# Causal mask, negation and row maximum of attention scores fused into one VectorE instruction per head and query tile, in place in PSUM

## What is computed

```python
scores = jnp.einsum('bqhd,bkhd->bhqk', qh, kh) / jnp.sqrt(jnp.float32(hd))
scores = jnp.where(causal[None, None, :, :], scores, -jnp.inf)
weights = jax.nn.softmax(scores, axis=-1)
out = jnp.einsum('bhqk,bkhd->bqhd', weights, vh).reshape(B, S, D)
```

## Time and profile before

| | us |
|---|---|
| median of 3 runs | 1448.44 |
| lowest and highest | 1437.71, 1454.72 |
| the profiled execution's own time | 1450.46 |
| its span in the trace | 1448.7 |
| TensorE matmuls busy | 1228.7 (85%) |
| TensorE weight loads busy | 1045.6 (72%) |
| VectorE busy | 904.6 (62%) |
| ScalarE busy | 557.8 (39%) |
| GpSimd busy | 626.0 (43%) |

### The profile page before, as it was taken

How to read it: one execution, slowest core, us unless ns; L and a number is a source line. 1 busy time by engine, 2 the same in 40 slices (tenths; PEclk the granted TensorE clock), 3 DMA queues, 4 the chain that set the end, 5 groups by cost and what they waited for, 6 DMA issues and landing times.

```text
span 1448.7 us, 33276 instructions
## 1 busy us (share of the span) xinstructions
PE 1228.7 (85%) x12722; PEld 1045.6 (72%) x12722; DVE 904.6 (62%) x2063; ACT 557.8 (39%) x959; POOL 626.0 (43%) x996
## 2 busy tenths in 40 slices
PE   1488999999999999999999997648997878979874
PEld 1366777777777777777777766548996768979874
DVE  2376767777877778688688685567874323434331
ACT  0124444443444443434434443234452334545431
POOL 3123333334544444444344443416326555645564
PEclk7799999999999999999999998769997889989987
DMA  3201112113223232232232212487666555857630
GB/s 113 83 19 49 47 38 72 48 51 111 89 83 102 82 101 84 82 110 81 82 104 79 86 63 76 157 301 249 234 239 175 178 178 178 269 196 260 207 127 26
DMA packets 84230, 177.73 MB, mean 123 GB/s; under 512 B 16370, under 2 KB 57594, under 8 KB 84070
## 3 DMA queue, kind: packets, MB, share of 16 engines
q1 hardware_dynamic: 70406, 146.73, 31.4%
q0 software_dynamic: 13664, 28.84, 5.6%
HBM read 128.96 MB, written 50.38 MB: 124 GB/s over the span
## 4 chain that ended last, share of the span: by engine, by line
PE 40%; DVE 20%; issue 14%; POOL 11%; ACT 6%; DMA 4%; SPq 3%; another core or an unknown queue 1%; POOLq 0%; DVEq 0%; ACTq 0%
PE h_ps L1615 9%; PE y_ps L1626 9%; DVE capped L974 4%; ACT PT L738 3%; PE round_banks L582 3%; POOL sorted_d L226 3%; DVE xn L990 3%; PE gen L502 3%; POOL PT L852 3%; DVE nm L978 2%; PE round_banks L555 2%; PE gen L544 2%; PE gen L511 2%; DVE nm L976 2%; POOL rstd L845 2%
## 5 line engine op out<-in xcount | busy, mean ns | idle before, releaser
L738 ACT ACTIVATE PT<-round_banks 128x1752 f32<-128x1752 f32 x96 | 156.6, 1632 | 174.8 <-PE round_banks L582 174.8
L852 POOL TENSOR_SCALAR_AFFINE_SELECT PT<-PT 128x512 f32<-128x512 f32 x192 | 117.7, 637 | 207.7 <-ACT PT L738 207.2
L1705 ACT ACTIVATE Gl<-h_ps,W 128x256 f32<-128x256 f32 x264 | 117.0, 474 | 233.5 <-PE h_ps L1615 165.7
L1626 PE MATMUL y_ps<-W,Gl 128*128 128x192 f32 x1056 | 194.0, 340 | 0.7 <-issue 0.7
L1615 PE MATMUL h_ps<-XH,Wh 128*128 128x256 f32 x528 | 156.7, 312 | 39.2 <-issue 25.3
L1626 PEld LDWEIGHTS y_ps<-W,Gl 128*128 128x128 f32 x1056 | 184.3, 201 | 1.3 <-issue 1.3
L1530 POOL DMA_INDIRECT out_dram<-Y,sid x88 | 94.7, 1077 | 154.3 <-DVE Y L1798 130.7
L502 PE MATMUL gen<-w_emb,xT 128*128 128x192 f32 (+1 forms) x768 | 141.0, 335 | 7.5 <-DMA ident<-in_ident_dram 7.5
L1615 PE MATMUL h_ps<-XH,Wl 128*128 128x256 f32 x528 | 146.5, 297 | 0.0
L1774 DVE TENSOR_TENSOR Wl<-W,Wh 128x768 fp32r<-128x768 f32 x88 | 84.2, 958 | 96.5 <-ACT Wh L1685 49.7
L1615 PEld LDWEIGHTS h_ps<-XH,Wh 128*128 128x128 f32 x528 | 108.4, 205 | 44.6 <-issue 35.4
(11 more groups left out here) (272 smaller groups left out, 2450.0 us busy)
## 6 DMA issues: line engine op xcount, KB each, us to landing
W<-in_experts_dram SPq DMA_DIRECT2D x44, 771.0 KB
W<-in_experts_dram SPq DMA_DIRECT2D x44, 672.0 KB
xT<-in_xT_dram SPq DMA_DIRECT2D x32, 591.0 KB
X<-sorted_d SPq DMA_DIRECT2D x35, 450.0 KB
stage<-rows_d SPq DMA_DIRECT2D x64, 224.0 KB
rows_d<-xn SPq DMA_DIRECT2D x32, 256.0 KB
rows_d<-h SPq DMA_DIRECT2D x32, 192.0 KB
out_dram<-h SPq DMA_DIRECT2D x32, 192.0 KB
```

Source lines behind the costliest of these rows:

```text
L738: act.activation(PT[(JG * b + j) % 2][:], R[:, :, 0:438], ACT.Exp, scale=SCALE).then_inc(exps, 1)
L852: pool.affine_select(x[:, :, at:at + P], x[:, :, at:at + P], [[0, GH], [1, P]], ALU.is_ge, 0.0, base=0, channel_multiplier=-1)
L1626: mm = pe.matmul(y_ps[t.par][:, k * D:(k + 1) * D], Gl[t.par][:, f, k * P:(k + 1) * P], W[t.i][:, W2O + f * D:W2O + (f + 1) * D], start=(f ...
L1705: act.activation(Gl[t.par][:, f, :], h_ps[f % 3][:, 0:ROWS], ACT.Gelu, bias=W[t.i][:, B1O + f:B1O + f + 1]).then_inc(g_ready, 1)
```

## The change

`reduce_max` no longer writes a masked copy. For each of the four heads and each of the two query tiles it issues one `tensor_tensor_reduce`: it adds the mask to the block of scores, multiplies by -1, writes the result back over the scores in the bank, and keeps the minimum in an accumulator that goes to one column of `nm`. The mask has 256 columns now, of which the first 128 are zero: tile 0 uses the last 128 and tile 1 all 256. `r_emptied` is incremented by the last of the eight. Tile 1's two blocks share one result, so L1189 goes, and in its place VectorE waits for its own T reduction and increments `nmax_ready`.

```diff
-        masks = sb("masks_f", [P, P])
+        masks = sb("masks_f", [P, 2 * P])
-        capped = sb("capped", [P, GH, 2, P])
...
                 x = nm[:, 12 * j:12 * j + 12].rearrange("p (h r) -> p h r", r=3)
-                blocks = R[:, :, 0:3 * P].rearrange("p h (r k) -> p h r k", k=P)
-                if j or b:
-                    dve.wait_ge(capped_read, JG * b + j)
-                dve.tensor_tensor(capped[:], blocks[:, :, 0:3:2, :],
-                                  masks[:].rearrange("p (a b k) -> p a b k", a=1, b=1).broadcast_to([P, GH, 2, P]), ALU.add).then_inc(capped_set, 1)
-                dve.tensor_reduce(x[:, :, 1], blocks[:, :, 1, :], AX.X, ALU.max, negate=True).then_inc(r_emptied, 1)
-                dve.wait_ge(capped_set, JG * b + j + 1)
-                dve.tensor_reduce(x[:, :, 0:3:2], capped[:], AX.X, ALU.max, negate=True).then_inc(capped_read, 1)
+                for i in range(GH):
+                    for r, lo, n in ((0, 0, P), (2, P, 2 * P)):
+                        block = R[:, i, lo:lo + n]
+                        ins = dve.tensor_tensor_reduce(block, block, masks[:, 2 * P - n:2 * P], -1.0, -BIG, ALU.add, ALU.min, x[:, i, r:r + 1])
+                ins.then_inc(r_emptied, 1)
...
-                    x = nm[:, 0:36].rearrange("p (h r) -> p h r", r=3)
-                    dve.wait_ge(r_emptied, 4 * b + 3)
-                    dve.wait_ge(capped_read, JG * b + JG)
-                    dve.tensor_tensor(x[:, :, 2], x[:, :, 1], x[:, :, 2], ALU.min).then_inc(nmax_ready, 1)
+                    dve.wait_ge(r_emptied, 4 * b + 4)
+                    dve.sem_inc(nmax_ready, 1)
...
-    o["masks"] = np.where(i[None, :] > i[:, None], BIG, 0.0).astype(np.float32)
+    o["masks"] = np.concatenate([np.zeros((P, P)), np.where(i[None, :] > i[:, None], BIG, 0.0)], 1).astype(np.float32)
```

More of the change, by code:

```diff
@@ L318, in attention @@
         r_filled, r_emptied = sem("r_filled"), sem("r_emptied")
-        capped_set, capped_read = sem("capped_set"), sem("capped_read")
         steps = sem("steps")
```

## The result

The changed kernel is slower: a median of 1480.1 us (five runs, 1473.8 to 1505.7) against 1450.5 us for the kernel before (five runs), a ratio of 1.021 with a 95% interval of 1.016 to 1.025. The forecast was 1483 us, within 1460 to 1560.

A forecast was written before the change was run, and what follows sets the result against it. TensorE was taken to bound the attention stage, VectorE counting where TensorE waits for it. The profiled 1450.5 us plus 34 for longer turns and 0.6 for the mask gave 1485, or 1483 against the median; range 1460 to 1560.

The forecast's parts named there:

- The banks are held longer: Each M round releases its banks 2.91 us after its start instead of 1.79, 1.12 us later.
- The round on VectorE: Eight fused instructions at 2.06 us plus read-outs at 0.80 make 2.86 us, 0.03 more than before.
- The read-out: One-element accumulator write into nm after each fused instruction, eight per round, taken at 0.10 us each.
- The write in place: Writing scores back to the banks instead of to SBUF: no cost taken, left to the bounds of the whole round.
- M0 is hidden: The longer hold at M0 costs nothing, covered by 1.87 us before S0; without that cover, 1.12 us a turn.
- S1 comes later by the whole extra hold: TensorE already waits for M1's banks at score round S1, so S1 starts 1.12 us later.
- T comes 1.1 us late: Tail round T waits for VectorE's M2 release, not the copy L902; about 1.1 us later, S1's delay included.
- 31 turns x 1.1 + 0.6: Total loss: 34 us from 31 longer attention turns, plus 0.6 us of waiting for the larger mask at the start.
- What would show it: Signs: fused rows about 0.285 and 0.42 us, S1 waiting 1.7 us, S1 to S1 27.8 us, T released by VectorE.
- No overlap: Rival: no VectorE instructions overlap, so a round takes 4.04 us; 121 us slower, 1569 us; chance 0.18.
- full read-outs: Rival: each read-out costs VectorE its full 0.15 us, so a round takes 3.3 us; 1511 us; chance 0.22.
- Not slower: Rival: read-outs cost VectorE's queue nothing, round 2.1 us, T 0.3 us earlier; 9.6 us gained, 1439 us; chance 0.10.

The follow-up runs named there:

- hold_late: Kernel before the change, with L976, the reduction that releases the banks, moved behind L978; the same three instructions; 1460.7 us, ratio 1.048 to the kernel before.
- fused_sbuf: Changed kernel with the fused instructions' full result written to SBUF instead of back over the scores; 1400.4 us, ratio 1.006 to the kernel before.
- fused_m0: Kernel before the change, with the fused instructions in the M0 rounds alone and the old three elsewhere; 1392.6 us, ratio 0.999 to the kernel before.
- after_again: The changed kernel unaltered, run again beside the kernel before for a second profile; 1422.4 us, ratio 1.020 to the kernel before.
- no_mask: Kernel before the change, with the mask left out of the maxima: one reduction straight from the banks, no copy; 1366.7 us, ratio 0.979.
- fused_m2: Kernel before the change, with the fused instructions in the M2 rounds alone and the old three elsewhere; 1435.8 us, ratio 1.031 to the kernel before.
- load_more: Kernel before the change, with one more 512-element reduction behind L978 in each M round, banks released as before; 1438.8 us, ratio 1.029.
- fused_m1: Kernel before the change, with the fused instructions in the M1 rounds alone and the old three elsewhere; 1404.9 us, ratio 1.010 to the kernel before.
- fused_m0_m2: Kernel before the change, with the fused instructions in the M0 and M2 rounds and the old three in M1; 1429.8 us, ratio 1.029.

## Why the prediction was right, point by point

- *TensorE bounds the attention stage, and VectorE counts where TensorE waits for it.* Right: VectorE's busy time fell by 7 us in 103 and the kernel got slower.
- *The banks are held longer; this is the term that counts.* Right: hold_late. The size was 2.91 us forecast against 2.60 to 2.63, so 0.8 us more than before and not 1.12.
- *The round on VectorE: 2.86 us.* It is 2.46 to 2.49. Two terms were mis-sized and cancelled in part. The read-out was taken at 0.10 us and costs the queue 0.02 us when the fused instruction writes to SBUF (0.21 us between starts, where 0.19 was worked out for the instruction alone). The write in place was taken at nothing and costs 0.04 us for each of eight instructions. The second is the larger fault: by fused_sbuf the in-place write carries some 20 of the 27 us, and the prediction left it to the bounds.
- *M0 is hidden.* Right in three turns of four. The 1.87 us were read in one turn; in every fourth there are only 0.37, and S0 came 0.54 us later. fused_m0 is at 0.999 because the same turn gets more than that back at M1.
- *S1 comes later by the whole extra hold.* Right in three turns of four: 0.82 us. In the fourth VectorE used to reach M1 late and is on time now, so S1 came 0.12 us sooner; hence the average of 0.58.
- *T comes 1.1 us late, now by VectorE; S1's delay lies inside it.* T follows M2's last read-out, as it did before in most turns. But the forecast let VectorE reach M2 as late as before and counted the hold once. In fact the round is shorter and M2 later, VectorE is hardly late, and the hold counts twice, less 0.90 us. T came 0.73 us later behind M1 in half of the turns, 1.17 in one of four, and 0.21 earlier in the one that M0 makes longer.
- *31 turns x 1.1 + 0.6 = 35 us.* Measured 0.83 us a turn and 27 to 30 us. That it came so near is in part luck: a hold that was taken 0.3 us too long, and counted once and not twice. With the forecast's own hold of 2.91 us counted twice, the sum would be 2 x 1.12 - 0.90 = 1.3 us a turn. No run bears out the 0.6 us for the larger mask: VectorE waits 33.0 us for the constants in after_again and 32.9 before, and the first M round's weight loads start between 69.6 and 72.2 us in all kept runs, the large mask having the earliest.
- *What would show it.* The rows are 0.32 and 0.47 us and not 0.285 and 0.42, S1 waits 1.38 us and not 1.7, and S1 to S1, in the same kinds of turn as 413.75 to 440.45 in the earlier trace rows, is 27.28 us (428.91 to 456.19) and not 27.8: every sign points the forecast way, and each is smaller than forecast but the rows.
- *The rivals.* No overlap, full read-outs: excluded by the starts 0.25 and 0.38 apart. The Trainium skill's rule in "VectorE: DVE Perf Modes", section "The DRAIN you can't avoid", taken strictly, would have each start wait for the pipe to empty; the read-outs start in the same hundredth as the next instruction. Its section "Two Vector instructions with no wait between them" counts the accumulator output as a second instruction that nothing holds back here, and the trace agrees. "Not slower" needed a round below about 2.3 us: fused_sbuf, at 2.22 us and a release at 2.30, is still 0.6% slower, so that point was set a little too high.

## What to carry to other kernels

An instruction that reads a single-buffered PSUM region costs twice: its time in its own queue, and the time until the region comes free, and the second is on the path wherever the next writer already waits, as often per turn as that happens: here twice. So ask of a fusion when the last read of the banks ends, not how many elements or busy microseconds it saves: here three instructions of which only two read the banks beat sixteen with less to do. Read the cover of a wait in every kind of turn, not in one. If a by-product isn't needed, writing it to SBUF rather than back over what it was read from was worth 1.5% here; and look first for the version that needs no second operand at all (no_mask, 2.1% faster than before).

## What the runs showed of the hardware that was not expected

The write back into PSUM in place: 322 and 467 ns against 283 and 419 to SBUF, and the read-out behind it 143 against 83.

The granted clock. From 92 to 881 us it was 1.00 throughout in the profile of before; most variants had stretches at 0.50 there, the 1.2 GHz level. In fused_m2, the stretches around one T, with the same columns as above:

```profile
191.00:194.00 3.00, 3.00 (x49) 2.32 (x48) 2.93 (x14) 0.92 (x2) 2.22 (x5) 1.00 0.00 0
194.00:197.00 3.00, 1.28 (x40) 0.70 (x32) 1.74 (x12) 0.40 (x1) 0.51 (x2) 0.82 0.01 3
197.00:200.00 3.00, 3.00 (x25) 2.59 (x14) 1.37 (x2) 0.59 (x1) 0.00 (x0) 0.50 0.00 0
200.00:203.00 3.00, 3.00 (x18) 2.46 (x21) 0.17 (x1) 1.36 (x3) 0.00 (x0) 0.50 0.02 5
203.00:206.00 3.00, 3.00 (x28) 2.96 (x21) 0.00 (x0) 1.98 (x2) 0.28 (x1) 0.50 0.01 3
```

And its weight loads there:

```profile
195.85 0.38 PEld L565 LDWEIGHTS round_banks<-tmask,identb 128*96 128x96 bf16 x4 [1.78 <-issue]
...
197.38 0.66 PEld L511 LDWEIGHTS gen<-ident,att 128*96 128x96 f32 x4 [0.87 <-issue]
```

TensorE's loads stood for 1.78 us, and as they began again at 195.85 the clock fell: 0.82 in the mean of that stretch, then 0.50 until about 206 us. The second pause, 0.87 us, lies behind the fall. The falls add up to 12 to 18 us in hold_late, load_more, fused_m2, fused_m1 and fused_m0_m2, and to 0.4 in after_again with its waits of 1.4 us. In fused_m1 S1 waits 2.32 us in six turns, and the clock falls behind each of the six; in the kernel before S1 waits 1.50 us in the same turns, and it never falls. But a wait doesn't decide it alone: in fused_m2 a fall at 527 us lies behind a wait of T of 1.24 us, while other waits of 1.24 to 1.45 us there left the clock at 1.00, and no_mask, the fastest, has 8.6 us of falls, at the start and the end of the stage. So in this kernel a longer wait can cost more than itself; what it costs is in the table of four turns, and what exactly sets it off no run here settles.
